# Differential attention: PE's shared-bank work placed between a slot's diagonal and its later scores

## The chip, the core and the metric

The kernel runs on one core of a Trainium2 chip. Its engines are PE (matmul), ACT (activation functions), DVE and POOL (elementwise work) and SP (which starts the DMAs); each takes its instructions in program order, and they wait for each other by semaphores. The metric is the device time of the whole kernel in microseconds, as a median of several runs; lower is better.

## What is computed

The reference is a stack of four layers over x of shape (16, 512, 128): differential attention, a grouped-query attention with a mixture of experts, eight blocks of linear attention, and a ternary feed-forward layer. Only the first is touched by the change:

```python
B, T, D = x.shape                      # 16, 512, 128; nh = 16, hd = 8
q = (x @ Wq.T).reshape(B, T, 2, nh // 2, hd)
k = (x @ Wk.T).reshape(B, T, 2, nh // 2, hd)
v = (x @ Wv.T).reshape(B, T, nh // 2, 2 * hd)
q, k = (_rms_norm(q), _rms_norm(k))
q, k = (_apply_rotary(q, cos, sin), _apply_rotary(k, cos, sin))
y1 = _causal_attn(q[:, :, 0], k[:, :, 0], v, scale)
y2 = _causal_attn(q[:, :, 1], k[:, :, 1], v, scale)
y = (y1 - lambda_full * y2).reshape(B, T, D)
return y @ Wproj.T
```

with x layer-normalised before and the result added to it. `_causal_attn` is softmax attention with a causal mask.

## The kernel before

`diff_attention` handles 16 batches of 512 tokens. The 16 heads of a batch are taken two at a time, so a batch has 8 slots, m = 0 to 7, and slot n = 8b + m + 1 of the whole stage is worked on in pass m of batch b. The scores of a slot are held transposed (keys on the partitions), in blocks of 128 by 128 at or above the causal diagonal:

- `score_diagonal(n)` (L1402, L1404) makes the eight diagonal blocks into two PSUM banks, SX. It waits until ACT has taken SX's last contents (`probs_x`).
- `score_later(n)` (L1416 to L1427) makes the remaining blocks, six matmuls, into three banks, SY. It waits for `probs_y`, that is for ACT's exponentials of the slot before.
- ACT: `exp_diagonal(n)` (L1566) and `exp_later(n)` (L1571) write exp of SX and of SY into a ring of six slots, PT. POOL masks the diagonal blocks (L1649).
- `weigh` (L1439) multiplies PT with V into the bank O, for a group of two slots: the blocks off the diagonal at even m, the diagonal ones at odd m. DVE copies O out (`copy_o`, L1822).

All else that needs PSUM goes through the two banks of M, the shared banks. A slot has one or two such uses on PE. Batch b's attention runs beside the projections of batches b + 1 and b + 2 (c and c2 in the code) and the output of batch b - 1 (p):

| m | PE's uses of M |
|---|---|
| 0 | `project_ks(c)` L1261, `turn_o2(p)` L1298 |
| 1 | `sum_q(c)` L1273, L1274 |
| 2 | `sum_k(c)` L1283, L1284, `turn_o3(p)` L1298 |
| 3 | `project_v(c)` L1291 |
| 4 | `turn_y(p)` L1341, `turn_o0(b)` L1298 |
| 5 | `project_out(p)` L1349, `turn_x(c2)` L1232 |
| 6 | `project_q(c2)` L1239, `turn_o1(b)` L1298 |
| 7 | `project_k(c2)` L1246, `project_qs(c2)` L1254 |

ACT empties some of these uses in an order of its own, written out by hand: `square` (L1526) in m = 6 and 7 and `rms` (L1532, L1535, Ln and Exp) in m = 1 and 2 stand between `exp_diagonal` and `exp_later`; `copy_v` (L1542, m = 3), `copy_yT` (L1548, m = 4) and `copy_xT` (L1520, m = 5) stand behind `exp_later`. The uses wait for their banks: `turn_y` for `copy_v`, `project_out` for `copy_yT`, `project_q` for `copy_xT`, `turn_x` for the combine of the group 0 on DVE (L1830), `turn_o2` for the sines on DVE (L1747). DVE's order is fixed as well: sines, combine(p,2), measure, `copy_o(p,3)`, splitting of q (L1754 to L1765), combine(p,3), splitting of k, `copy_o(b,0)`, centre (L1731), combine(b,0), `add_out`, and so on.

Of the kernel before, what the change touches and what calls it, by code (L numbers as in the profile page):

```python
# [1086 lines left out]
def diff_attention(nc, C, XT, G, NB):  # L1087
# [13 lines left out]
    with ExitStack() as ctx:  # L1101
# [119 lines left out]
        def pe_program(pe):  # L1221
# [35 lines left out]
            def project_ks(c):  # L1257
                if c:
                    pe.wait_ge(cos_done[K], c + 1)
                    pe.wait_ge(sq_ready[K], c + 1)  # L1260
                pe.matmul(lead(c, 1), w[:, 3, :], xnT[:, :], start=True, stop=True  # L1261
                          ).then_inc(turned_filled[K], 1)

            def sum_q(c):
                if c:
                    pe.wait_ge(sin_done[Q], c + 1)
                else:
                    pe.wait_ge(heads_ready, 1)
                    pe.wait_ge(sq_ready[Q], 1)
                if c >= 2:  # L1270
                    pe.wait_ge(o_used, 4 * (c - 2) + 3)
                pe.wait_ge(sq_split[Q], c + 1)
                pe.matmul(lead(c, 2), heads[:, :], sqs[:, 0, Q, :], start=True, stop=False)  # L1273
                pe.matmul(lead(c, 2), heads[:, :], sqs[:, 1, Q, :], start=False, stop=True  # L1274
                          ).then_inc(ss_filled[Q], 1)

            def sum_k(c):
                if c:
                    pe.wait_ge(ss_taken[Q], c + 1)
                else:  # L1280
                    pe.wait_ge(sq_ready[K], 1)
                pe.wait_ge(sq_split[K], c + 1)
                pe.matmul(lead(c, 3), heads[:, :], sqs[:, 0, K, :], start=True, stop=False)  # L1283
                pe.matmul(lead(c, 3), heads[:, :], sqs[:, 1, K, :], start=False, stop=True  # L1284
                          ).then_inc(ss_filled[K], 1)
# [25 lines left out]
            def turn_o1(b):  # L1311
                if b:
                    pe.wait_ge(out_done, b)
                else:
                    pe.wait_ge(v_taken, 2)
                turn_o(b, 1)

            def turn_o2(p):
                if p + 2 <= NB:
                    pe.wait_ge(sin_done[Q], p + 3)  # L1320
                else:
                    pe.wait_ge(o_used, 4 * p + 2)
                turn_o(p, 2)
# [40 lines left out]
            def g_project_qs():  # L1364
                pe.wait_ge(o_used, 4 * (NB - 2) + 2)
                pe.matmul(M[:, 1, :], G["wq"][:, 1, :], xnT[:, :], start=True, stop=True
                          ).then_inc(turned_filled[Q], 1)

            def g_sum_k():
                pe.wait_ge(sin_done[Q], NB + 1)  # L1370
                pe.wait_ge(o_used, 4 * (NB - 2) + 3)
                pe.wait_ge(g_kk_done, 1)
                pe.matmul(M[0:32, 1, :], G["pair_sum"][:, :], rotK, start=True, stop=True
                          ).then_inc(g_k_summed, 1)
# [9 lines left out]
            def operands(n, i):  # L1384
                pair, par = n % 8, (n // 8) % 2
                return (qT[64 * i:64 * i + KR, par, pair, :], kT[64 * i:64 * i + KR, par, pair, :])

            def score_diagonal(n):

                if n % 4 == 0:  # L1390
                    pe.wait_ge(loaded[Q][n // 4 % 2], 32 * (n // 8 + 1))
                    pe.wait_ge(loaded[K][n // 4 % 2], 32 * (n // 8 + 1))
                if n:
                    pe.wait_ge(probs_x, n)
                else:
                    pe.wait_ge(cos_done[K], 1)
                    pe.wait_ge(sq_ready[K], 1)
                    pe.wait_ge(sin_done[K], 1)
                (qa, ka), (qb, kb) = operands(n, 0), operands(n, 1)
                for j in range(NT):  # L1400
                    t = slice(j * P, (j + 1) * P)
                    pe.matmul(SX[:, 0, t], ka[:, t], qa[:, t], start=True, stop=True,  # L1402
                              skip_group_check=True)
                    last = pe.matmul(SX[:, 1, t], kb[:, t], qb[:, t], start=True, stop=True,  # L1404
                                     skip_group_check=True)
                last.then_inc(x_ready, 1)

            def score_later(n):

                if n:  # L1410
                    pe.wait_ge(probs_y, n)
                else:
                    pe.wait_ge(ss_taken[K], 1)
                    pe.wait_ge(v_taken, 1)
                (qa, ka), (qb, kb) = operands(n, 0), operands(n, 1)
                pe.matmul(SY[:, 1, 0:256], ka[:, P:2 * P], qa[:, 2 * P:SEQ], start=True, stop=True,  # L1416
                          skip_group_check=True).then_inc(shared_half, 1)
                pe.matmul(SY[:, 2, 0:384], kb[:, 0:P], qb[:, P:SEQ], start=True, stop=True,
                          skip_group_check=True)
                pe.matmul(SY[:, 0, 0:384], ka[:, 0:P], qa[:, P:SEQ], start=True, stop=True,  # L1420
                          skip_group_check=True)
                pe.matmul(SY[:, 2, 384:512], kb[:, 2 * P:3 * P], qb[:, 3 * P:SEQ], start=True,
                          stop=True, skip_group_check=True)
                pe.matmul(SY[:, 0, 384:512], ka[:, 2 * P:3 * P], qa[:, 3 * P:SEQ], start=True,
                          stop=True, skip_group_check=True)
                pe.wait_ge(shared_half, n + 1)
                pe.matmul(SY[:, 1, 256:512], kb[:, P:2 * P], qb[:, 2 * P:SEQ], start=True, stop=True,  # L1427
                          skip_group_check=True).then_inc(y_scored, 1)
# [31 lines left out]
            for b in range(NB + 1):  # L1460
                p, c, c2 = b - 1, b + 1, b + 2
                tail, now, then, next_but_one = b >= 1, b < NB, c < NB, c2 < NB
                for m in range(8):
                    n = 8 * b + m + 1
                    group = 4 * b + m // 2 - 1
                    weighing = 0 <= group < 4 * NB
                    if n < 8 * NB:
                        score_diagonal(n)
                        score_later(n)
                    if m == 0 and then:  # L1470
                        project_ks(c)
                    if m == 0 and tail:
                        turn_o2(p)
                    if m == 1 and then:
                        sum_q(c)
                    if m == 2 and then:
                        sum_k(c)
                    if m == 2 and c == NB:
                        g_sum_k()
                    if m == 2 and tail:  # L1480
                        turn_o3(p)
                    if m == 3 and then:
                        project_v(c)
                    if m == 3 and c == NB:
                        g_project_v()
                    if m == 4 and tail:
                        turn_y(p)
                    if m == 4 and now:
                        turn_o0(b)
                    if m == 5 and tail:  # L1490
                        project_out(p)
                    if m == 5 and c2 <= NB:
                        turn_x(c2)
                    if m == 6 and next_but_one:
                        project_q(c2)
                    if m == 6 and c2 == NB:
                        g_project_q()
                    if m == 6 and now:
                        turn_o1(b)
                    if m == 7 and next_but_one:  # L1500
                        project_k(c2)
                        project_qs(c2)
                    if m == 7 and c2 == NB:
                        g_project_kk()
                        g_project_qs()
                    if weighing and m % 2 == 0:
                        pe.wait_ge(probs_y, 2 * group + 2)
                        if group:
                            pe.wait_ge(o_copied, group)
                        weigh(group, EARLY[0] + EARLY[1])  # L1510
                    if weighing and m % 2 == 1:
                        pe.wait_ge(masked, 2 * group + 2)
                        weigh(group, DIAG[0] + DIAG[1]).then_inc(av_ready, 1)
# [2355 lines left out]
```

## Time and profile before

| | us |
|---|---|
| median of 3 runs | 3155.96 (3155.24 to 3159.12) |
| profiled execution | 3165.76 |
| its span, first to last instruction | 3164.0 |
| PE busy | 2882.8 (91% of the span) |
| DVE busy | 2482.6 (78%) |
| ACT busy | 2326.2 (74%) |
| POOL busy | 2104.2 (67%) |
| mean granted clock of PE | 0.954 |

The stage of the change is the first one; its last addition to x ends at 523.48 us. The other stages are the same code in both kernels. A timeline row gives the start, the length, the engine and line, and in brackets the time for which the engine did nothing before the instruction, with the instruction that ended the wait.

### The profile page before, as it was taken

Reading aid. Unit: us, or ns where it says so; the run is one execution under the profiler, and the core shown is the slowest. Engines: PE = TensorE matmul, PEld = TensorE weight load, DVE = VectorE, ACT = ScalarE, POOL = GpSimd, SP = SyncE. Lnnn points to the kernel's source line nnn. Section 1 sums busy time; section 2 is a strip of 40 time slices with the busy share of each in tenths; the row PEclk is TensorE's granted clock in tenths of the full one; section 3 lists DMA queues with packets and bytes.
Section 4 is the critical chain, followed back from the end, with each engine's and each line's share of the span. In section 5 each row is a group of like instructions: output and inputs, shape, how many; then the busy total and the mean of one; then the engine's idle time right before and its main releaser. Section 6 shows DMA issues by size and latency. Waiting matters only on the chain. (4 is left out here: it accounts for less than half of the span.)

```text
span 3164.0 us, 66212 instructions
## 1 busy us (share of the span) xinstructions
PE 2882.8 (91%) x22258; PEld 1871.3 (59%) x22258; DVE 2482.6 (78%) x6944; ACT 2326.2 (74%) x3601; POOL 2104.2 (67%) x2402
## 2 busy tenths in 40 slices
PE   6999997788998888789579999999999999999979
PEld 3555554344444444678246666666666666666668
DVE  5777776788888875567468888888888888888867
ACT  5888883466666667444289999999999999999833
POOL 5666673346555543577657888788877888788745
PEclk8999997799999999899789999999999999999989
DMA  4544534223322330685400000000000000000001
GB/s 121 131 108 112 129 92 91 59 62 69 69 57 60 72 70 19 191 271 158 128 1 1 17 1 17 1 7 11 6 12 1 17 1 17 1 17 1 1 14 41
DMA packets 151509, 178.31 MB, mean 56 GB/s; under 512 B 18619, under 2 KB 122784, under 8 KB 151076
## 3 DMA queue, kind: packets, MB, share of 16 engines
q1 hardware_dynamic: 142084, 157.14, 19.2%
q0 software_dynamic: 9088, 16.94, 1.6%
q8 instruction: 179, 2.93, 0.4%
q14 instruction: 158, 1.29, 0.1%
HBM read 99.82 MB, written 75.95 MB: 56 GB/s over the span
## 5 line engine op out<-in xcount | busy, mean ns | idle before, releaser
L3380 PE MATMUL lb_FF<-lb_h,lb_w 128*128 128x512 f32 x1024 | 502.0, 592 | 0.0
L3609 DVE TENSOR_SCALAR lb_z<-lb_M,lb_mv,lb_rstd 128x128 f32<-128x128 f32 x1024 | 344.9, 398 | 3.3 <-POOL lb_rstd L3534 3.0
L3497 ACT ACTIVATE lb_h<-lb_H,lb_prm 128x512 f32<-128x512 f32 x512 | 327.5, 699 | 2.6 <-PE lb_H L3371 2.6
L3534 POOL TENSOR_TENSOR lb_rstd<-lb_rstd,half 128x4 f32<-128x4 f32 x256 | 260.8, 1019 | 37.2 <-issue 1.3
L3365 PE MATMUL lb_H<-lb_x1s,lb_w 128*128 128x512 f32 x512 | 273.0, 533 | 0.0
L3380 PEld LDWEIGHTS lb_FF<-lb_h,lb_w 128*128 128x128 f32 x1024 | 193.5, 189 | 89.9 <-issue 61.1
L3601 DVE BATCH_NORM_STATS2 lb_stats<-lb_M 128x6 f32<-128x128 f32 x1024 | 226.9, 284 | 15.5 <-PE lb_M L3324 9.0
L1649 POOL TENSOR_SCALAR_AFFINE_SELECT da_PT<-da_PT 128x1024 f32<-128x1024 f32 x128 | 149.1, 1165 | 133.4 <-ACT da_PT L1566 133.3
L3366 PE MATMUL lb_H<-lb_x1s,lb_w 128*128 128x512 f32 x512 | 203.3, 397 | 0.0
L3371 PE MATMUL lb_H<-lb_x1s,lb_w 128*128 128x512 f32 x512 | 202.7, 397 | 0.1
L3552 POOL CAST lb_x1s<-lb_x 128x512 fp32r<-128x512 f32 x128 | 78.3, 611 | 173.7 <-DVE lb_x L3634 173.7
L2631 POOL DMA_INDIRECT moe_ys<-moe_y,moe_dest x156 | 159.0, 1019 | 50.5 <-issue 44.9
L794 DVE TENSOR_REDUCE ga_bm<-ga_S 128x8 f32<-128x1024 f32 x128 | 156.5, 1222 | 42.5 <-PE ga_S L379 41.4
L791 DVE TENSOR_REDUCE ga_bm<-ga_S 128x8 f32<-128x1024 f32 x128 | 156.0, 1219 | 42.4 <-PE ga_S L379 41.8
L1571 ACT ACTIVATE da_PT<-da_SY 128x1536 f32<-128x1536 f32 x128 | 184.8, 1443 | 0.0
L1566 ACT ACTIVATE da_PT<-da_SX 128x1024 f32<-128x1024 f32 x128 | 131.0, 1023 | 67.4 <-PE da_SX L1404 67.1
L3545 POOL TENSOR_TENSOR lb_xs<-H,lb_xs 128x512 fp32r<-128x512 f32 x126 | 167.8, 1332 | 18.1
L3555 POOL TENSOR_TENSOR lb_x1s<-lb_x,lb_x1s 128x512 fp32r<-128x512 f32 x128 | 163.5, 1277 | 20.8 <-issue 20.8
L3566 POOL TENSOR_TENSOR lb_y<-lb_ao,H 128x512 f32<-128x512 f32 x128 | 165.4, 1292 | 16.0 <-ACT lb_ao L3484 14.0
L1439 PE MATMUL da_O<-da_PT,da_V 128*32 128x128 f32 (+2 forms) x3584 | 174.6, 335 | 0.0
L3578 POOL TENSOR_TENSOR lb_y<-lb_ff,lb_x 128x512 f32<-128x512 f32 x128 | 165.1, 1290 | 8.5 <-PE lb_M L3324 5.3
L3478 ACT ACT_TABLE_LOAD x131 | 168.1, 1283 | 2.3
(514 smaller groups left out, 8860.8 us busy)
## 6 DMA issues: line engine op xcount, KB each, us to landing
moe_w<-experts_dram SPq DMA_DIRECT2D x39, 384.0 KB, 3.2
da_qT<-da_stq SPq DMA_DIRECT2D x64, 192.0 KB, 4.1
da_kT<-da_stk SPq DMA_DIRECT2D x64, 192.0 KB, 3.8
moe_x<-moe_xs SPq DMA_DIRECT2D x39, 260.0 KB, 3.6
tc_g<-moe_ys SPq DMA_DIRECT2D x32, 256.0 KB, 3.5
ga_q<-ga_stq SPq DMA_DIRECT2D x20, 384.0 KB, 5.8
lb_split<-moe_parts SPq DMA_DIRECT2D x8, 896.0 KB, 6.4
da_stq<-da_parts SPq DMA_DIRECT2D x16, 384.0 KB, 2.4
```

Source lines behind the costliest of these rows:

```text
L1439: last = pe.matmul(O[32 * c:32 * c + 32, q0:q0 + cols], V[:, (n // 4) % 2, j, 2 * (n % 4) + c % 2, :], PT[:, (2 * n + c // 2) % RING, c % ...
L1571: act.activation(PT[:, n % RING, :, 512:HEAD_COLS], SY[:, :, :].rearrange("p a n -> p (a n)").rearrange("p (i n) -> p i n", i=2), ACT.Exp, ...
L3365: pe.matmul(H[:, k % 2, :], w1[:, 0, k, :], x1s[:, 0, :], start=True, stop=False)
L3366: pe.matmul(H[:, k % 2, :], w1[:, 1, k, :], x1s[:, 0, :], start=False, stop=False)
L3371: pe.matmul(H[:, k % 2, :], w1[:, 0, k, :], x1s[:, 1, :], start=False, stop=True).then_inc(h_filled, 1)
L3380: pe.matmul(FF[:, :], w2[:, k, :], h[:, k, :], start=(k == 0), stop=(k == KC - 1)).then_inc(ff_filled, 1)
L3478: act.preload_act_table_set("gelu_apprx_tanh_and_others")
L3497: act.activation(h[:, k, :], H[:, k % 2, :], ACT.Gelu_apprx_tanh, bias=col(FB1 + k, i)).then_inc(h_ready, 1)
L3534: pool.tensor_tensor(out[:, :], out[:, :], C["half"][:, 0:NT], ALU.pow).then_inc(done, 1)
L3545: pool.tensor_tensor(part_of_x(i, 1), state(i), part_of_x(i, 0).bitcast(F32), ALU.subtract).then_inc(xs_ready, 1)
L3601: v.bn_stats(stats[:, t, :], M[:, t * P:(t + 1) * P])
L3609: last = v.tensor_scalar(z[:, t, :], M[:, t * P:(t + 1) * P], mv[:, t, 0:1], rstd[:, t:t + 1], ALU.subtract, ALU.mult)
```

## The change

In each slot `score_later(n)` moves from directly behind `score_diagonal(n)` to behind the slot's uses of M; `weigh` stays last. ACT, DVE, POOL and SP keep their orders.

```diff
--- before.py
+++ after.py
@@ -1466,7 +1466,6 @@
                     weighing = 0 <= group < 4 * NB
                     if n < 8 * NB:
                         score_diagonal(n)
-                        score_later(n)
                     if m == 0 and then:
                         project_ks(c)
                     if m == 0 and tail:
@@ -1503,6 +1502,8 @@
                     if m == 7 and c2 == NB:
                         g_project_kk()
                         g_project_qs()
+                    if n < 8 * NB:
+                        score_later(n)
                     if weighing and m % 2 == 0:
                         pe.wait_ge(probs_y, 2 * group + 2)
                         if group:
```

In m = 5 of a batch, PE's rows were (L1404 ends the diagonal scores, L1349 is `project_out`, L1232 is `turn_x`, L1439 is `weigh`):

```order
L1404 MATMUL da_SX<-da_qT,da_kT 128x128
L1416 MATMUL da_SY<-da_qT,da_kT 128x256
L1418 MATMUL da_SY<-da_qT,da_kT 128x384
L1420 MATMUL da_SY<-da_qT,da_kT 128x384
L1422 MATMUL da_SY<-da_qT,da_kT 128x128
L1424 MATMUL da_SY<-da_qT,da_kT 128x128
L1427 MATMUL da_SY<-da_qT,da_kT 128x256
L1349 MATMUL da_M<-da_wout,da_yT 128x128 x4
L1232 MATMUL da_M<-ident,da_xn 128x128 x4
L1439 MATMUL da_O<-da_PT,da_V 32x128 x16
```

and are now:

```order
L1404 MATMUL da_SX<-da_qT,da_kT 128x128
L1349 MATMUL da_M<-da_wout,da_yT 128x128 x4
L1232 MATMUL da_M<-ident,da_xn 128x128 x4
L1416 MATMUL da_SY<-da_qT,da_kT 128x256
L1418 MATMUL da_SY<-da_qT,da_kT 128x384
L1420 MATMUL da_SY<-da_qT,da_kT 128x384
L1422 MATMUL da_SY<-da_qT,da_kT 128x128
L1424 MATMUL da_SY<-da_qT,da_kT 128x128
L1427 MATMUL da_SY<-da_qT,da_kT 128x256
L1439 MATMUL da_O<-da_PT,da_V 32x128 x16
```

The six later scores moved behind `project_out` and `turn_x`.

In m = 2, from the last of the later scores to the first of `weigh` (`sum_k`, L1283 and L1284, and `turn_o3`, L1298):

```order
L1427 MATMUL da_SY<-da_qT,da_kT 128x256
L1283 MATMUL da_M<-da_sqs,da_heads 128x512
L1284 MATMUL da_M<-da_sqs,da_heads 128x512
L1298 MATMUL da_M<-ident,da_oT 128x128 x4
L1439 MATMUL da_O<-da_PT,da_V 32x384 x4
```

and now, from the last of the diagonal scores to the first of the later ones:

```order
L1404 MATMUL da_SX<-da_qT,da_kT 128x128
L1283 MATMUL da_M<-da_sqs,da_heads 128x512
L1284 MATMUL da_M<-da_sqs,da_heads 128x512
L1298 MATMUL da_M<-ident,da_oT 128x128 x4
L1416 MATMUL da_SY<-da_qT,da_kT 128x256
```

`sum_k` and `turn_o3` now stand ahead of the wait that the first later score (L1416) has.

ACT from the norm of m = 2 to the copy of m = 5, the same in both kernels (L1532 and L1535 are the Ln and Exp of the norm, L1542, L1548 and L1520 the three copies):

```order
L1532 ACTIVATE da_rs<-da_M,rms_eps 128x512
L1535 ACTIVATE da_rs<-da_rs 128x512
L1571 ACTIVATE da_PT<-da_SY 128x2x768
L1566 ACTIVATE da_PT<-da_SX 128x2x512
L1571 ACTIVATE da_PT<-da_SY 128x2x768
L1542 ACTIVATE da_V<-da_M 128x32x16
L1566 ACTIVATE da_PT<-da_SX 128x2x512
L1571 ACTIVATE da_PT<-da_SY 128x2x768
L1548 ACTIVATE da_yT<-da_M 128x512
L1566 ACTIVATE da_PT<-da_SX 128x2x512
L1571 ACTIVATE da_PT<-da_SY 128x2x768
L1520 ACTIVATE da_xnT<-da_M 128x512
```

Nothing moved here: each copy stands behind the later exponentials (L1571) of its slot.

## Rows read from the trace of the kernel before

**Rows 1.** Busy times: two neighbouring batches, then thirteen. Columns: stretch, length; PE, PEld, DVE, ACT, POOL busy; clock; DMA.
```profile
270.65:300.02 29.37, 26.82 (x389) 16.73 (x388) 22.20 (x42) 24.11 (x26) 19.57 (x18) 1.00 0.44 117
240.51:270.65 30.14, 28.23 (x389) 17.25 (x388) 21.50 (x42) 24.23 (x26) 19.46 (x18) 0.94 0.46 117
62.79:449.86 387.07, 357.21 (x5045) 220.99 (x5044) 283.79 (x533) 314.20 (x326) 253.84 (x234) 0.97 0.45 115
```
**Rows 2.** Waits on PE, 60 to 450 us: in total, times, longest (us).
```profile
PE da_SY L1416 <- ACT da_PT L1571: 23.8, 20, 1.5
```
**Rows 3.** Timeline of PE: start us, length us, instruction [idle before it].
```profile
268.31 0.63 PE L1232 MATMUL da_M<-ident,da_xn 128*128 128x128 f32 x4 [0.42 <-DVE da_u L1830]
...
270.65 1.12 PE L1239 MATMUL da_M<-da_xnT,da_w 128*128 128x512 f32 x2
...
279.03 0.60 PE L1298 MATMUL da_M<-ident,da_oT 128*128 128x128 f32 x4
...
282.43 1.08 PE L1439 MATMUL da_O<-da_PT,da_V 128*32 128x128 f32 x32
...
285.33 0.28 PE L1416 MATMUL da_SY<-da_qT,da_kT 48*128 48x256 bf16 x1 [1.49 <-ACT da_PT L1571]
...
289.44 0.28 PE L1416 MATMUL da_SY<-da_qT,da_kT 48*128 48x256 bf16 x1 [0.63 <-ACT da_PT L1571]
...
289.99 1.16 PE L1291 MATMUL da_M<-da_w,da_xnT 128*128 128x128 f32 x8
...
292.87 0.66 PE L1341 MATMUL da_M<-ident,da_y 128*128 128x128 f32 x4
...
293.89 1.50 PE L1439 MATMUL da_O<-da_PT,da_V 128*32 128x384 f32 x24
...
297.68 0.63 PE L1232 MATMUL da_M<-ident,da_xn 128*128 128x128 f32 x4 [0.42 <-DVE da_u L1830]
...
298.24 1.08 PE L1439 MATMUL da_O<-da_PT,da_V 128*32 128x128 f32 x32
```
**Rows 4.** Timeline of ACT in the same batch.
```profile
281.43 1.03 ACT L1566 ACTIVATE da_PT<-da_SX 128x1024 f32<-128x1024 f32 x1 [1.34 <-PE da_SX L1404]
...
282.54 0.69 ACT L1532 ACTIVATE da_rs<-da_M,rms_eps 128x512 f32<-128x512 f32 x1
...
283.84 1.43 ACT L1571 ACTIVATE da_PT<-da_SY 128x1536 f32<-128x1536 f32 x1
...
289.28 1.02 ACT L1566 ACTIVATE da_PT<-da_SX 128x1024 f32<-128x1024 f32 x1
...
290.19 1.45 ACT L1571 ACTIVATE da_PT<-da_SY 128x1536 f32<-128x1536 f32 x1
...
291.52 0.61 ACT L1542 ACTIVATE da_V<-da_M 128x512 f32<-128x512 f32 x1
...
298.35 0.60 ACT L1520 ACTIVATE da_xnT<-da_M 128x512 f32<-128x512 f32 x1 [0.21 <-PE da_M L1232]
```
**Rows 5.** Timeline of DVE in this batch and the one before.
```profile
253.44 0.69 DVE L1822 COPY da_oT<-da_O 128x512 f32<-128x512 f32 x1
...
262.86 0.69 DVE L1822 COPY da_oT<-da_O 128x512 f32<-128x512 f32 x1 [1.83 <-PE da_O L1439]
...
277.42 0.69 DVE L1822 COPY da_oT<-da_O 128x512 f32<-128x512 f32 x1 [0.51 <-PE da_O L1439]
...
278.03 0.68 DVE L1747 TENSOR_TENSOR da_rotB<-da_M,da_rope 128x512 f32<-128x512 f32 x1
...
283.58 0.69 DVE L1822 COPY da_oT<-da_O 128x512 f32<-128x512 f32 x1
...
284.19 0.78 DVE L1754 TENSOR_TENSOR da_rotA<-da_rotA,da_rs 128x512 f32<-128x512 f32 x1
...
289.00 1.64 DVE L1754 TENSOR_TENSOR da_rotA<-da_rotA,da_rs 128x512 f32<-128x512 f32 x1
...
292.23 0.69 DVE L1822 COPY da_oT<-da_O 128x512 f32<-128x512 f32 x1 [0.36 <-PE da_O L1439]
```

## The prediction

> **What bounds the kernel now.** I first read which part of the span the change can touch: only the first stage, differential attention, to about 524 us of the 3164.0 us span. There I took the busy times of single batches [rows 1]. In a batch without any half-clock stretch PE is busy 26.82 of 29.37 us, ACT 24.11, DVE 22.20, POOL 19.57. No engine is full, so order and waits set the length. Then I read who waits for whom on PE [rows 2]: one wait is large, the later scores of a slot (L1416) for the exponentials of the slot before (L1571), 23.8 us in 20 places, the longest 1.5 us. The timelines of one clean batch on PE, ACT and DVE [rows 3 to 5] show where it is. I number the slots of a batch m = 0 to 7; a batch of shared-bank work is followed from m = 6 (project_q, L1239) to the next m = 6. The wait falls in m = 2 (285.33, idle 1.49) and m = 3 (289.44, idle 0.63), and one smaller wait, of 0.42 us, in m = 5, where turn_x (L1232) waits for DVE (297.68). Everywhere else PE runs without a pause.
>
> Why just m = 2: in m = 1 and 2 ACT has the norm's Ln and Exp (1.30 us from 282.54 to 283.84) in front of L1571, so the exponentials run late, and PE stands with its shared-bank uses of m = 2 still to do. The change puts those uses into that wait. So far it looks like a gain; what has to be counted is what the same order does in the other six slots, where PE didn't wait.
>
> **The change, step by step.** No instruction is added or removed. In every slot the later scores (0.55 us of PE, from 289.44 to 289.99) go behind the slot's shared-bank uses. The other pieces of a slot are the weighting matmuls (1.01 or, on even m, 1.43: 1.08 of row 298.24 and 1.50 of row 293.89, less the 0.07 by which the last one runs on) and the diagonal scores (0.22, what is left of the 2.34 between 268.31 and 270.65 after 0.56, 1.01 and 0.55), so a slot starts 0.77 before its first shared-bank use in the old order. I carry the clean batch through the new order, starting at the turn_x of 268.31, which stays where it is, and keep "shift" for new time minus old time. A result of PE or ACT reaches a waiting engine 0.05 us after its end (the 0.63 us turn of 297.68 ends at 298.31, the copy starts at 298.35).
>
> m = 5 to 6. Old: ACT does L1571 of m = 5 while PE waits for turn_x, so copy_xT follows the turn at once, and project_q starts 2.34 us after turn_x (268.31 to 270.65). New: the later scores stand behind turn_x, ACT's L1571 behind them, and copy_xT behind L1571, as ACT's order is unchanged. That is 0.56 (297.68 to 298.24) + 0.63 until the scores are out (their 0.55 and a run-on of 0.08) + 0.05 + 1.33 (290.19 to 291.52) + 0.60 + 0.05 = 3.22 us. Shift of project_q: +0.88, and PE idles in m = 6, where it did not.
>
> m = 7 only carries this: uses +0.88, weighting matmuls and next slot +1.43, since the scores now lie behind the uses. The DVE copies of O therefore come 1.43 late.
>
> m = 0. turn_o2 (old 279.03) needs sines(Q), which DVE does behind copy_o: copy at 277.42 + 1.43, sines 0.61 later and 0.69 long, so 280.20, against 279.91 by PE alone. Shift +1.17. The slot after it starts +1.72.
>
> m = 1. The first exponentials start at 281.43 + 1.72 = 283.15; 0.91 later (289.28 to 290.19) Ln and Exp, whose sums are there by then, 1.30, so L1571 at 285.36 (old 283.84, +1.52), its end (1.43 long) visible at 286.84. PE's weighting matmuls start at 282.43 + 1.17 + 0.55 = 284.15 and end so that m = 2 starts at 285.16; copy_o(p,3), old 283.58, also shifts by 1.72 and starts at 285.30.
>
> m = 2. Here the gain is. sum_k and turn_o3 run inside the wait; the later scores start at 286.84, then directly the weighting matmuls: 286.84 + 0.55 + 1.43 = 288.82 for m = 3. The old start of m = 3 is 289.99 - 0.55 - 0.63 (the idle time) - 0.4 (diagonal scores to their last end) = 288.41. The shift has gone from +1.72 to +0.41: 1.31 us back. On ACT the diagonal exponentials of m = 2 follow L1571 at 286.69, and L1571 of m = 2 comes 0.91 + 1.30 later, at 288.90; its 1.44 end, visible, at 290.39.
>
> m = 3. project_v lies inside the wait, the later scores start at 290.39 (old 289.44), and with 0.55 and 1.01 m = 4 starts at 291.95, old 292.10: 0.56 more back. PE is level with the old order here.
>
> m = 4. turn_y must wait for copy_v, since it writes the bank of M that copy_v reads. ACT's copy_v stands behind L1571 of m = 3, which starts 0.91 after the one of m = 2 has let ACT go (288.90 + 1.33): 291.14; copy_v at 292.47, 0.61 long, visible 293.13; PE is ready at 292.17. In the old order copy_v ended at 292.13 and turn_y was at 292.87, with the later scores ahead of it. Cost 0.96. With 1.02 for both turns (292.87 to 293.89), 0.55 and 1.43, m = 5 starts at 296.13.
>
> m = 5. The same on ACT: copy_yT stands behind L1571 of m = 4, whose scores now come behind turn_y and turn_o0 (294.15), so 0.68 later L1571, 294.83 + 1.33 + 0.60 + 0.05 = 296.81 for project_out, PE ready at 296.35: 0.46 idle. project_out takes 1.09, like project_v (289.99, 1.16 with the run-on). It ends at 297.90: by PE and ACT alone turn_x is at +0.22.
>
> DVE decides last. turn_x needs the combine behind centre, and DVE's work from copy_o(p,3) on has no pause that it must have. Its length without its own idle time is 14.10 - 0.36 = 13.74 us in the clean batch (283.58 to 297.68), and 14.87 - 1.83 = 13.04 in the one before (253.44 to 268.31) [rows 3, 5]. From 285.30 this gives 298.34 to 299.04, so +0.66 to +1.36 per batch. The spread comes from DVE instructions that run beside POOL: L1754 took 0.78 us at 284.19 and 1.64 us at 289.00. I take +0.9, nearer to the shorter chain, since the shorter chain was measured where POOL's mask of m = 3 came at another moment than in the clean batch, as it will in the new order too.
>
> The number of batches is 14 (turn_x for 2 to 15): 14 x 0.9 = +12.6; ends 14 x 0.66 = +9.2 and 14 x 1.36 = +19.0. The transfers between batches are no term: their stores hang on DVE's splits, shifted by the same 1 to 2 us, and the loads are used two slots or more later.
>
> The clock. From the first of 13 whole batches to the last (62.79 to 449.86) 387.07 us passed; 13 x 29.37 would be 381.8. The 5.3 us more are in batches like the second of [rows 1], 30.14 us at a mean clock of 0.94 (2.4 GHz with a stretch at 1.2). The half-clock stretch comes right behind the 1.5 us wait of m = 2. The new order breaks that wait up: the largest left is 0.95. I credit two thirds of the 5.3, -3.5; bounds 0 and -5.3 (PE stands 3.2 us per batch in the new order by the steps above, against 2.5 in the old, which argues against the whole).
>
> Sum: +12.6 - 3.5 = **+9.1 us**. The profiled execution of before took 3165.76 us (span 3164.0 and 1.8 around it), so its like would take 3174.9. That execution is 0.3% above the median of the timed ones, 3155.96; on the median I predict **3165 us**.
>
> The Trainium skill ("SBUF — State Buffer", section "SBUF: two separate sides") says that DVE and POOL share one port pair under an exclusive lock, and the later one blocks fully. The 1.64 against the 0.78 us of the L1754 at 284.19 agrees. By this rule the chain could also lose its blocked pieces in the new phase; then DVE would be out of the way, which is the second rival.
>
> The same skill ("TensorE: Matmul & The Clock Gate", section "What's actually happening") says that the slow clock is the default and activity releases it. By that rule a fuller m = 2 keeps the clock and a broken-up batch may lose it elsewhere; the traces here show only the first half.
>
> **Rivals.**
> 1. Faster. The 1.31 + 0.56 us regained in m = 2 and 3 stay, because the waits of m = 4 and 6 for ACT's copies don't bind: 14 x 1.87 = -26, with the clock about -30: 3126 us; half of it would be 3141. For it: this is PE's one large wait [rows 2]. Against: three copies on ACT (copy_v, copy_yT, copy_xT) stand behind L1571 in the same program order. Chance 0.07.
> 2. No difference. DVE's chain falls below the PE and ACT path (+0.22) or the clock gives all 5.3 us back: 14 x 0.22 - 5.3 = -2.2, 14 x 0.66 - 5.3 = +3.9: 3154 to 3160. For it: 0.86 us of the clean chain is the one long L1754 (1.64 against 0.78). Chance 0.27.
> 3. Forecast, +5 to +16: 3161 to 3172. Chance 0.53.
> 4. Much slower. A DVE instruction more is caught beside POOL (another 0.86, as 1.64 against 0.78): +1.36 + 0.86 = +2.2 per batch, 14 x 2.2 - 3.5 = +27: 3183. It decides as soon as the chain is longer than 13.74. Chance 0.13.
>
> What this kernel's timing can tell from no change is about 0.2%, 6.3 us. Rivals 2 and the low end of 3 lie within it: faster 0.07, same 0.30, slower 0.63. Range 3153 to 3179: it leaves out rival 1 and the far part of rival 4.
>
> **What would show it.** Right: PE's wait at L1416 shrinks to some 0.3 us in m = 2 and 3; new waits at turn_y (L1341) for ACT L1542 of 0.9 us and at project_q (L1239) for ACT L1520 of 0.9 us, 14 or so each; turn_x still waits for DVE; ACT now waits before L1571 for L1427, which it hardly did; batches of 30.0 to 30.8 us. Wrong: no wait at L1239, batches under 29.4, or half-clock stretches as frequent as before with batches at 30.3 (then only the clock term fails). If POOL's or DVE's mean durations change by more than 0.1 us each, the DVE term is the one that was mis-sized.

## The result: slower by 0.45%, and the profile after

| | before | changed |
|---|---|---|
| median of 5 runs each, us | 3156.47 | 3170.68 |
| lowest to highest | 3155.24 to 3161.16 | 3170.28 to 3179.54 |
| ratio | | 1.0045 (95%: 1.0029 to 1.006) |
| profiled execution, span | 3164.0 | 3177.8 |
| batch without half-clock stretch | 29.37 | 30.69 |
| thirteen batches | 387.07 | 399.95 |
| last addition of the stage starts | 522.8 | 535.4 |

The change costs 14.2 us; 3165 was predicted, with 3153 to 3179 as the range. The interval of the ratio means 9 to 19 us, so the forecast of +9.1 lies at its low end. Of the 13.8 us by which the spans differ, 12.6 lie in the first stage.

A clean batch and the thirteen whole batches of the changed kernel, to be laid beside [rows 1] (stretch, length; PE, PEld, DVE, ACT, POOL busy; clock; DMA):

```profile
307.02:337.71 30.69, 28.14 (x389) 16.56 (x389) 21.34 (x41) 23.89 (x26) 18.95 (x18) 1.00 0.46 114
60.51:460.46 399.95, 366.58 (x5045) 215.53 (x5045) 277.17 (x534) 310.66 (x326) 246.58 (x234) 1.00 0.44 112
```

PE executes the same instructions as in 26.82 busy us before, and the profile counts as much idle time in both batches (29.37 - 26.82 = 2.55 and 30.69 - 28.14 = 2.55). So the whole 1.32 us of the longer batch stand as busy. I read them as waits all the same: a row's length runs on past the moment at which the next instruction could have started, and where PE has to wait, that run-on hides a part of it. The turn_y of 298.19 below is followed 1.01 us later by turn_o0, of which the profile calls 0.38 idle. In the old order the distance was 0.49 us (292.87 to 293.36):

```profile
293.36 0.60 PE L1298 MATMUL da_M<-ident,da_oT 128*128 128x128 f32 x4
```

The clock over thirteen batches is 1.00 where it was 0.97. No half-clock stretch starts in them any more; only the end of one reaches into the first (60.51, mean clock 0.97, 31.57 us long). The stage is longer all the same.

Who waits for whom on PE, 62 to 462 us (us in all, times, longest), against [rows 2]. From 1506 on, lines are one higher than before, so L1572 is the L1571 of before, L1543 the L1542, L1521 the L1520:

```profile
PE da_M L1341 <- ACT da_V L1543: 11.3, 13, 0.9
PE da_M L1239 <- ACT da_xnT L1521: 8.9, 13, 0.7
PE da_M L1298 <- DVE da_oT L1823: 5.0, 12, 0.7
PE da_M L1349 <- ACT da_yT L1549: 3.5, 13, 0.3
PE da_M L1232 <- DVE da_u L1831: 3.2, 13, 0.3
PE da_SY L1416 <- ACT da_PT L1572: 0.3, 1, 0.3
```

The one large wait is gone (0.3 us instead of 23.8), and there are five others, one of each in nearly every batch, which before were not there or were one of 0.42 us. They add up to 31.9 us. Before, all that the profile lists added up to 29.6 (23.8, 5.5 at turn_x and 0.3), so the sum alone would not show the loss: the hidden parts of the waits are missing in it. On ACT the wait has changed sides:

```profile
ACT da_PT L1572 <- PE da_SY L1427: 73.7, 65, 1.8
ACT da_PT L1567 <- PE da_SX L1404: 8.2, 26, 0.3
```

Before, ACT waited 51.5 us for the diagonal scores and not at all for the later ones. Now it waits 73.7 us for the later scores.

PE's timeline of one clean batch, first the turn_x that starts it, then the later scores and uses of M from m = 2 on, to be laid beside [rows 3]:

```profile
273.13 0.63 PE L1232 MATMUL da_M<-ident,da_xn 128*128 128x128 f32 x4 [0.25 <-DVE da_u L1831]
...
291.82 0.28 PE L1416 MATMUL da_SY<-da_qT,da_kT 48*128 48x256 bf16 x1
...
295.36 0.28 PE L1416 MATMUL da_SY<-da_qT,da_kT 48*128 48x256 bf16 x1
...
298.19 0.63 PE L1341 MATMUL da_M<-ident,da_y 128*128 128x128 f32 x4 [0.87 <-ACT da_V L1543]
299.20 0.63 PE L1298 MATMUL da_M<-ident,da_oT 128*128 128x128 f32 x4 [0.38 <-DVE da_oT L1823]
...
302.40 1.16 PE L1349 MATMUL da_M<-da_wout,da_yT 128*128 128x128 f32 x8 [0.27 <-ACT da_yT L1549]
303.81 0.63 PE L1232 MATMUL da_M<-ident,da_xn 128*128 128x128 f32 x4 [0.25 <-DVE da_u L1831]
304.37 0.28 PE L1416 MATMUL da_SY<-da_qT,da_kT 48*128 48x256 bf16 x1
...
307.02 1.13 PE L1239 MATMUL da_M<-da_xnT,da_w 128*128 128x512 f32 x2 [0.69 <-ACT da_xnT L1521]
```

In m = 2 and 3 the later scores start without a stop of PE that the profile shows. Each use of M from turn_y in m = 4 to project_q in m = 6 has a wait. The length of each slot, from its first diagonal score to that of the next slot, shows where the batch wins and loses:

| us | m = 6 | 7 | 0 | 1 | 2 | 3 | 4 | 5 | batch |
|---|---|---|---|---|---|---|---|---|---|
| before, from 269.88 | 3.70 | 3.71 | 3.71 | 2.44 | 4.97 | 3.68 | 3.23 | 3.93 | 29.37 |
| changed, from 305.93 | 4.57 | 3.80 | 4.06 | 2.55 | 3.58 | 3.12 | 4.83 | 4.18 | 30.69 |

m = 2 and 3 give 1.95 us back, m = 4 loses 1.60, m = 6 0.87, and the other four 0.80 together. On ACT, the same batch as the timeline above:

```profile
296.10 1.45 ACT L1572 ACTIVATE da_PT<-da_SY 128x1536 f32<-128x1536 f32 x1
297.43 0.61 ACT L1543 ACTIVATE da_V<-da_M 128x512 f32<-128x512 f32 x1
...
300.41 1.45 ACT L1572 ACTIVATE da_PT<-da_SY 128x1536 f32<-128x1536 f32 x1 [1.46 <-PE da_SY L1427]
301.76 0.59 ACT L1549 ACTIVATE da_yT<-da_M 128x512 f32<-128x512 f32 x1
...
305.03 1.45 ACT L1572 ACTIVATE da_PT<-da_SY 128x1536 f32<-128x1536 f32 x1 [1.76 <-PE da_SY L1427]
306.37 0.59 ACT L1521 ACTIVATE da_xnT<-da_M 128x512 f32<-128x512 f32 x1
```

Each copy (297.43, 301.76, 306.37) stands directly behind the later exponentials of its slot, and these had to wait 1.46 and 1.76 us for scores that PE makes last. And on DVE, from copy_o(p,3) to combine, beside [rows 5]:

```profile
290.36 0.69 DVE L1823 COPY da_oT<-da_O 128x512 f32<-128x512 f32 x1 [1.97 <-PE da_O L1439]
290.97 1.33 DVE L1755 TENSOR_TENSOR da_rotA<-da_rotA,da_rs 128x512 f32<-128x512 f32 x1
...
293.68 1.37 DVE L1766 CAST da_parts<-da_rotB 128x512 bf16<-128x512 f32 x1
...
296.36 1.57 DVE L1755 TENSOR_TENSOR da_rotA<-da_rotA,da_rs 128x512 f32<-128x512 f32 x1
...
298.37 0.68 DVE L1823 COPY da_oT<-da_O 128x512 f32<-128x512 f32 x1
...
300.25 2.75 DVE L1732 TENSOR_SCALAR da_xn<-XT,da_mv,da_rstd 128x128 f32<-128x128 f32 x4
```

DVE has no idle time here between 290.36 and turn_x at 303.81: 13.45 us, between the 13.04 and 13.74 of before.

### The profile page after: what moved, and what is told of

It reads as the page before. It is cut to its first block and busy times, and to the rows that moved or that the text cites. A ratio compares the mean times of both kernels' runs of the same rounds, so it can differ in the third digit from the quotient of the medians.

```text
span 3177.8 us, 66212 instructions
## 1 busy us (share of the span) xinstructions
PE 2891.9 (91%) x22258; PEld 1864.3 (59%) x22258; DVE 2473.5 (78%) x6944; ACT 2322.1 (73%) x3601; POOL 2094.2 (66%) x2402
## 5 line engine op out<-in xcount | busy, mean ns | idle before, releaser
L1572 ACT ACTIVATE da_PT<-da_SY 128x1536 f32<-128x1536 f32 x128 | 185.2, 1447 | 92.2 <-PE da_SY L1427 92.1
L1650 POOL TENSOR_SCALAR_AFFINE_SELECT da_PT<-da_PT 128x1024 f32<-128x1024 f32 x128 | 141.8, 1108 | 144.5 <-ACT da_PT L1567 144.5
L3567 POOL TENSOR_TENSOR lb_y<-lb_ao,H 128x512 f32<-128x512 f32 x128 | 165.1, 1290 | 16.3 <-ACT lb_ao L3485 14.2
L1439 PE MATMUL da_O<-da_PT,da_V 128*32 128x128 f32 (+2 forms) x3584 | 167.4, 325 | 0.0
```

The source lines that it names most:

```text
L1439: last = pe.matmul(O[32 * c:32 * c + 32, q0:q0 + cols], V[:, (n // 4) % 2, j, 2 * (n % 4) + c % 2, :], PT[:, (2 * n + c // 2) % RING, c % ...
L1572: act.activation(PT[:, n % RING, :, 512:HEAD_COLS], SY[:, :, :].rearrange("p a n -> p (a n)").rearrange("p (i n) -> p i n", i=2), ACT.Exp, ...
```

## The experiments

The time of the kernel before varied between 3153 and 3171 us over the chips on which these ran, so each run is read by its ratio to the runs of before on its own chip, and by its batch: the distance between two project_q starts without a half-clock stretch. It is 29.37 us before and 30.69 with the change. In most runs it repeats within 0.03 us. In f1, f2 and f3 it does not, because there PE also waits up to 1.4 us at the diagonal scores of m = 7: the 28.75 and 28.76 of f1 and f3 are the three batches of thirteen without that wait and without a half-clock stretch, and for f2 the middle one is given. So the thirteen whole batches of each profiled execution stand beside it, with the number of them that have a half-clock stretch of their own.

| run | batch, us | thirteen, us | with half clock | ratio to before (95%) |
|---|---|---|---|---|
| before | 29.37 | 387.07 | 6 | 1 |
| the change | 30.69 | 399.95 | 0 | 1.0045 (1.0029 to 1.0060) |
| e1, moved in m = 2, 3 | 29.83 | 392.27 | 3 | 1.0008 (0.9993 to 1.0023) |
| e2, moved in m = 5 | 30.29 | 398.09 | 5 | 1.0047 (1.0031 to 1.0062) |
| e3, moved in all but m = 5 | 29.38 | 383.45 | 1 | 0.9995 (0.9979 to 1.0011) |
| e4, change, copy_xT ahead | 29.92 | 389.91 | 1 | 1.0021 (1.0005 to 1.0037) |
| e8, moved in m = 7, 0 | 29.82 | 396.34 | 10 | 1.0027 (1.0017 to 1.0036) |
| f4, moved in m = 4 | 29.37 | 388.34 | 7 | 0.9992 (0.9980 to 1.0004) |
| f1, before, short mask | 28.75 | 384.79 | 7 | 0.9953 (0.9934 to 0.9971) |
| e6, change, short mask | 29.68 | 386.09 | 0 | 0.9975 (0.9962 to 0.9987) |
| e5, m = 2, 3, short mask | 27.57 | 359.54 | 0 | 0.9882 (0.9864 to 0.9901) |
| e7, m = 2, 3, third later | 29.83 | 392.58 | 3 | 1.0010 (0.9999 to 1.0022) |
| f3, before, centre early | 28.76 | 381.93 | 5 | 0.9994 (0.9980 to 1.0008) |
| f2, m = 2, 3, centre early | 28.43 | 371.45 | 0 | 0.9951 (0.9938 to 0.9964) |

### Which slots gain and which lose

Theory: the gain is in m = 2 and 3, the loss where ACT's copies follow the later exponentials. The five runs below differ from before only in the slots in which the scores are moved:

```diff
                     if n < 8 * NB:
                         score_diagonal(n)
-                        score_later(n)
+                        if not (m in (2, 3)):
+                            score_later(n)
...
+                    if n < 8 * NB and (m in (2, 3)):
+                        score_later(n)
                     if weighing and m % 2 == 0:
```

with `m == 5` in e2, `m != 5` in e3, `m in (7, 0)` in e8 and `m == 4` in f4.

**e1, m = 2 and 3 alone.**

> The later scores are moved only in m = 2 and 3, where PE waited. Theory (the gain and the loss sit in different slots): m = 2 and 3 give back 1.3 + 0.5 us, of which the waits of DVE and of ACT's copies behind them take about half, since turn_x hangs on DVE's chain; a batch takes 28.5 us (29.37 before), 14 x 0.9 = 12.6 us, and the half-clock stretches of the stage go as well, 5 us: 3139 us, between 3134 and 3146. Rival (any use of M ahead of the scores makes the exponentials late, or the chain on DVE sets the batch whatever PE does): no batch shorter than 29.3 us, 3151 us or more.

A batch of 29.83 us, longer than before and far from 28.5; the time itself does not differ clear of noise (1.0008). The rival was right in its second half, that DVE's chain sets the batch. PE's largest wait in this run:

```profile
PE da_M L1232 <- DVE da_u L1833: 20.6, 13, 1.6
```

1.6 us in each of 13 batches at turn_x. DVE and POOL in one batch show why (lines are two or three higher than before: L1757 is L1754, L1762 L1759, L1734 L1731, L1645 L1642, L1652 L1649). DVE:

```profile
252.71 0.69 DVE L1825 COPY da_oT<-da_O 128x512 f32<-128x512 f32 x1
...
258.14 1.64 DVE L1757 TENSOR_TENSOR da_rotA<-da_rotA,da_rs 128x512 f32<-128x512 f32 x1
259.88 1.14 DVE L1762 CAST da_parts<-da_rotA 128x512 bf16<-128x512 f32 x1
...
262.82 3.64 DVE L1734 TENSOR_SCALAR da_xn<-XT,da_mv,da_rstd 128x128 f32<-128x128 f32 x4
```

POOL at the same time:

```profile
258.05 1.19 POOL L1645 TENSOR_TENSOR da_parts<-da_rotB,da_parts 128x512 bf16<-128x512 f32 x1
259.21 1.52 POOL L1652 TENSOR_SCALAR_AFFINE_SELECT da_PT<-da_PT 128x1024 f32<-128x1024 f32 x1
262.99 1.19 POOL L1645 TENSOR_TENSOR da_parts<-da_rotB,da_parts 128x512 bf16<-128x512 f32 x1 [2.25 <-DVE da_parts L1768]
264.13 2.25 POOL L1652 TENSOR_SCALAR_AFFINE_SELECT da_PT<-da_PT 128x1024 f32<-128x1024 f32 x2
```

The cast of 259.88 took 1.14 us beside a mask (0.43 when alone), the product of 258.14 took 1.64 beside `third` (0.80 in the other place of the same batch), and the four instructions of centre took 3.64 beside `third` and two masks, where they took 2.75 before. The chain from copy_o(p,3) (252.71) to turn_x (267.27) is 14.56 us long without a pause. By gaining on PE and ACT in m = 2 and 3 the kernel moved a second mask onto centre. The gain could not come through in any case but by a shorter chain: from turn_x (237.44) to copy_o(p,3) it is 15.27 us, as before, for m = 2 and 3 do not lie in this part, and 15.27 + 14.56 = 29.83.

**e2, m = 5 alone.**

> Moved only in m = 5, behind turn_x. Theory: project_q waits for copy_xT, which stands behind the later exponentials (L1571), whose scores now stand behind turn_x: +0.88 us per batch, batch 30.2 to 30.4 us, half-clock stretches as before, 14 x 0.9 = +12.6: 3169 us. Rival (no single slot costs; the loss is the sum of small delays on DVE beside POOL): under +0.3 per batch, 3156 to 3160.

30.29 us, as the theory had it: +0.92 per batch. The wait at turn_x is 0.87 in place of 0.42, and that of m = 2 is as large as before:

```profile
PE da_M L1232 <- DVE da_u L1833: 11.3, 13, 0.9
...
PE da_SY L1416 <- ACT da_PT L1574: 27.0, 34, 1.5
```

**e3, all slots but m = 5.**

> The change in every slot but m = 5. Theory: the wait of project_q goes (0.7 to 0.9 us), turn_x still comes late by DVE's chain: batch 29.4 to 29.8 us against 30.69, with the half-clock stretches gone 3151 to 3158 us. Rival (DVE's chain alone sets the batch of the change): the batch stays near 30.7 and the time near 3170.

29.38 us, at the edge of what was expected: 1.31 less than the change. Without the move in m = 5 the clean batch is as long as before, and the time is too (0.9995): the 1.95 us that m = 2 and 3 give back are lost in the other slots, most of them (1.60) in m = 4. The profile shows no wait at turn_x, but DVE still releases it: turn_x follows the end of the combine by 0.15 us as in the change, and 15.92 (264.67 to 280.59) + 13.45 (280.59 to 294.04) = 29.37.

**e8, m = 7 and 0 alone.**

> Moved only in m = 7 and 0. Theory: turn_o2 waits for the sines behind the late copy_o, and every slot whose diagonal scores are followed by a use of M takes 0.08 us longer on PE: +0.35 us per batch, 29.7 us, ratio 1.001 to 1.002 with the half-clock stretches as before. Rival (nothing is lost outside m = 4 to 6): batch 29.4, ratio 1.000.

A clean batch is 29.82 us, a little over the expected 29.7. But the time rose by more than that, 1.0027 where at most 1.002 was expected. The granted clock over the stage:

```profile
62.00:462.00 400.00, 372.14 (x5097) 224.25 (x5092) 267.21 (x536) 318.37 (x329) 247.22 (x235) 0.96 0.45 114
```

The half-clock stretch that follows the wait of m = 2 came in 10 of the 13 batches instead of 6, and such batches are 30.6 us long. That part was not expected.

**f4, m = 4 alone.**

> Moved only in m = 4. In the whole change PE waits 0.87 us at turn_y for copy_v. Theory: that wait exists only because PE comes early out of m = 2 and 3; alone, copy_v has ended when PE comes, so batch 29.3 to 29.5 us and ratio 0.999 to 1.001. Rival (the slot costs by itself, as m = 5 does): batch 30 or more.

29.37 us: no loss, and at turn_y only four waits of at most 0.2 us. The wait of 0.87 us at turn_y exists only where PE comes out of m = 2 and 3 early.

### The copy on ACT

**e4, the whole change with copy_xT ahead.**

```diff
+                    if m == 5 and c2 <= NB:
+                        copy_xT(c2)
                     if n < 8 * NB:
                         exp_later(n)
...
-                    if m == 5 and c2 <= NB:
-                        copy_xT(c2)
```

> The whole change, with ACT's copy_xT of m = 5 ahead of that slot's later exponentials. Theory: the copy follows the turn at once, project_q starts 0.7 us earlier than in the change, batch 29.9 to 30.0 us (30.69), 3158 to 3161 us. Rival (what costs is that the scores themselves stand behind turn_x, whatever the copy does): batch 30.5 or more, 3168 or more.

29.92 us: 0.77 of the 1.32 us is the one copy that stands behind exp_later. The rival is out. The ratio, 1.0021, has a wide interval (1.0005 to 1.0037).

### How much is DVE beside POOL

The mask of a slot was cut to one block of four in three kernels (three of four diagonal blocks stay unmasked):

```diff
                 d = PT[:, n % RING, :, 0:512].rearrange("p i (j q) -> p i j q", j=NT)
-                pool.affine_select(d, d, [[0, 2], [0, NT], [1, P]], ALU.is_ge, 0.0, base=0,
+                d = d[:, :, 0, :]
+                pool.affine_select(d, d, [[0, 2], [1, P]], ALU.is_ge, 0.0, base=0,
```

**e5, m = 2 and 3 alone.**

> Moved only in m = 2 and 3, and POOL masks one of the four diagonal blocks of a slot (the other three stay unmasked: part of the computation is left out). Theory: in m = 2 and 3 alone, the batch of 29.83 us is DVE's chain from copy_o(p,3) to turn_x, 14.57 us long, in which centre takes 3.64 us beside two masks of POOL and the split of k 1.64 + 1.14 beside other POOL work. With short masks the chain is 12.5 to 13.5 us, turn_x hardly waits, batch 28.3 to 28.9 us; ratio to before 0.992 to 0.996. Rival (something else than DVE beside POOL holds turn_x back): batch 29.5 or more, ratio 0.999 or more.

27.57 us and 0.9882, below the expected 28.3 and 0.992. The split of k runs at 0.68 and 0.43 us and centre at 2.06. This is the largest effect of the study: 2.26 us per batch against e1.

**e6, the whole change.**

> The whole change with the same short mask (three of four diagonal blocks unmasked). Theory: DVE's waits at turn_o0 (0.38) and turn_x (0.25) go, the waits for ACT's copies (copy_v, copy_yT, copy_xT) stay: batch 30.0 to 30.3 us against 30.69, ratio to before 1.001 to 1.003. If the whole loss were DVE beside POOL, the batch would fall under 29.4 and the ratio below 1.0.

29.68 us, 0.3 below what was expected, so the collisions weigh more than I thought. The ratio missed too: 0.9975, under 1, where 1.001 to 1.003 was expected; what that means can only be said with the control, f1. The slot m = 4 falls from 4.83 to 4.25 us, as turn_o0 no longer waits for DVE. But the waits for ACT's copies are all still there, unchanged in size:

```profile
PE da_M L1341 <- ACT da_V L1543: 11.3, 13, 0.9
PE da_M L1239 <- ACT da_xnT L1521: 8.9, 13, 0.7
PE da_M L1349 <- ACT da_yT L1549: 3.5, 13, 0.3
```

**f1, the kernel before.**

> The kernel before with the short mask (one of four diagonal blocks masked), the control for the two runs with it, whose batches are 29.68 us (the whole change) and 27.57 us (m = 2 and 3 alone). Theory: before, DVE was hardly in the way (0.42 us at turn_x), and the half-clock stretches stay: batch 28.8 to 29.1 us. Then the order of the whole change costs 0.6 to 0.9 us per batch with DVE out of the way, and the order in m = 2 and 3 gives 1.2 to 1.5 us. Rival (without the collisions on DVE the whole change is no loss): batch 29.6 or more.

28.75 us in a clean batch. So with the collisions reduced the whole change still costs 29.68 - 28.75 = 0.93 us of its 1.32 in clean batches, and the move in m = 2 and 3 alone gains 28.75 - 27.57 = 1.18.

For the time this is weaker. Only three of the thirteen batches of f1 are clean: seven have a half-clock stretch, and in seven PE waits up to 1.3 us at the diagonal scores; e6 has neither. All thirteen take 384.79 us in f1 and 386.09 in e6, 1.3 us apart, where with whole masks they are 12.9 apart. The intervals of the two ratios, 0.9953 (to 0.9971) and 0.9975 (from 0.9962), overlap. That the order alone makes the kernel slower with short masks is therefore shown for the clean batch and not for the time.

**e7, another place for `third`.** As e1, and POOL's third(c, K) is put behind the mask of m = 4 (`if m == 3 and c < NB` becomes `m == 4`).

> Moved only in m = 2 and 3, and POOL's third(c, K) comes behind the mask of m = 4 instead of the mask of m = 3. POOL waited 2.25 us for the split of k with that mask's data ready; now it masks in that time. Theory: centre meets one POOL instruction less, 2.75 us instead of 3.64, batch 28.9 to 29.0 us, ratio 0.996 to 0.998. Rival: the batch stays at 29.8, or the later third makes the transfers of k late (a wait of PE for them in m = 7).

29.83 us, as in e1. The collision was not avoided but moved. DVE in this run:

```profile
293.33 1.61 DVE L1766 TENSOR_TENSOR da_rotB<-da_rotA,da_parts 128x512 f32<-128x512 f32 x1
...
295.36 2.73 DVE L1734 TENSOR_SCALAR da_xn<-XT,da_mv,da_rstd 128x128 f32<-128x128 f32 x4
```

Centre takes 2.73 us, as hoped, but now the subtraction in front of it (L1766) takes 1.61 instead of 0.69, because it meets the mask that was brought forward.

### A version that beats both

In f2 and f3 DVE measures and centres x one batch earlier, in the idle time that it has around project_q and project_k, so that centre is no longer between copy_o(p,3) and turn_x.

```diff
                 if now:
                     copy_o(b, 1)
+                if b + 3 < NB:
+                    measure(b + 3)
                 if next_but_one:
                     cosines(c2, Q)
                 if now:
                     combine(b, 1)
+                if b + 3 < NB:
+                    centre(b + 3)
                 if next_but_one:
                     cosines(c2, K)
```

The old places keep only what runs beside batch 0; POOL's rsqrt_stats goes to m = 6, and the load of x behind store_q of the batch two earlier.

**f2, with the scores moved in m = 2 and 3.**

> Moved only in m = 2 and 3, and DVE measures and centres the x of a batch one batch earlier, in its idle time of m = 6 and 7 (with POOL's rsqrt behind the mask of m = 6 and the load of x earlier), so that centre is not between copy_o(p,3) and turn_x. Nothing is left out. Theory: that chain falls from 14.57 to about 11 us and turn_x waits no more; batch 27.9 to 28.4 us against 29.37 before; with 14 batches and 5 us of half clock 16 to 25 us saved, ratio 0.992 to 0.996. Rival: centre in m = 7 holds back cosines(c2, K), and with it project_ks and copy_o(b, 2), by as much: batch 29 or more.

**f3, with the scores not moved.**

> The same early centre in the kernel before, later scores not moved, the control for the run above. Theory: only the 0.42 us at turn_x can go, the waits of m = 2 and 3 stay: batch 29.0 to 29.3 us, ratio 0.998 to 1.000. Then most of the gain of the run above is the move of the scores.

f2 is the fastest kernel of the study that computes everything: 0.9951 of before, 0.994 to 0.996, and the only one of those whose interval lies clear of 1 on this side. f3 has three clean batches of 28.76 us, better than the 29.0 expected, but its time is at 0.9994: the wait of m = 2 is still there, five batches have a half-clock stretch, and eight have a wait of up to 1.0 us at the diagonal scores. Over thirteen batches f3 takes 381.93 us and f2 371.45, so 29.38 and 28.57 per batch: with centre out of the way the move in m = 2 and 3 gives 0.81 us per batch. How much of it is clock and how much waiting can't be told from the clean batches, since f2 has only one without the wait at the diagonal scores (27.80 us; the others run from 28.04 to 29.24). In f2 centre's four instructions take 1.12 us in all but one of the thirteen, where DVE meets no POOL instruction:

```profile
292.08 1.12 DVE L1736 TENSOR_SCALAR da_xn<-XT,da_mv,da_rstd 128x128 f32<-128x128 f32 x4
```

What PE waits for in f2:

```profile
PE da_SX L1402 <- issue: 9.8, 13, 1.4
PE da_SY L1416 <- ACT da_PT L1574: 8.6, 29, 0.3
PE da_M L1232 <- DVE da_u L1835: 2.8, 1, 2.8
```

turn_x waits once only, and behind the thirteen batches (2.8 us). What remains is up to 1.4 us at the diagonal scores in twelve of the thirteen, without a releaser in the profile. The loads of q and k are one candidate: a load of k was issued at 286.44 and such loads take 4.1 us to land, against diagonal scores at 292.67. This was not tested, and the cause stays open.

## Why the prediction was right

Direction, range and mechanism held; the size was 14 us where 9 were forecast. Step by step:

- **m = 5 to 6, copy_xT.** 3.22 us from turn_x to project_q were worked out; 303.81 to 307.02 is 3.21. e2 (+0.92) and e4 (-0.77) show it alone, e3 (-1.31) what the move in m = 5 costs in the whole change.
- **m = 2 and 3.** PE's wait for L1571 is gone as said. The steps put 1.31 + 0.56 us into the two slots; they are 1.39 + 0.56 shorter. e1 shows that the batch keeps nothing of it while DVE's chain is in the way. With short masks it keeps 1.18 (e5 against f1, clean batches).
- **m = 4.** turn_y's wait: 0.96 forecast, 0.87 measured. But the slot lost 1.60 us, not 0.96: the steps had no wait at turn_o0, which starts 1.01 us behind turn_y instead of 0.49, as it waits for DVE's copy_o(b,0). In e6, where DVE comes in time, the slot loses 1.02. project_out's wait, 0.46 forecast, is 0.27, as PE comes to it later. f4 confirms that turn_y's wait needs the early PE.
- **DVE decides last.** True, and here is the term that was mis-sized. PE and ACT alone were put at +0.22; e6, whose turn_x waits no more for DVE, is at 29.68 - 29.37 = +0.31. The chain was right: 13.45 us, inside the 13.04 to 13.74, though 0.17 longer than the 13.28 that +0.9 stands for. Its start was not: copy_o(p,3) follows turn_x by 290.36 - 273.13 = 17.23 us, 1.96 more than before (283.58 - 268.31 = 15.27), where 1.72 was worked out. Each slot in which a use of M follows the diagonal scores takes about 0.08 us more on PE (the first use stands 0.3 us behind the first diagonal score, where the later scores stood 0.23 behind it), three times between turn_x and copy_o. So 1.96 - 0.65 (14.10 - 13.45) = +1.31 per batch and not +0.9. The upper end, +1.36, held.
- **The clock.** -3.5 was credited, with -5.3 as the bound. In the thirteen batches no half-clock stretch starts any more, so the whole 5.3 came back and not two thirds: 1.8 us more than credited, which hid a part of the mis-sized term. Their sum: 13 x 1.32 - 5.3 = 11.9, measured 12.9. The last 1.0 is in two batches: 0.88 in the first (31.57 us), into which the end of a half-clock stretch reaches and whose project_q takes 2.01 us instead of 1.13, and 0.35 in one (31.04 us) whose turn_o0 waits 0.74 us for DVE instead of 0.38; one batch is 0.19 shorter.
- **DVE beside POOL.** The long DVE instructions (0.68 to 1.64, 0.43 to 1.14, 0.69 to 1.61 us) stand beside POOL's in every trace, and they shrink when POOL's masks do. The rule of the Trainium skill ("SBUF — State Buffer", section "SBUF: two separate sides") that the later one is blocked agrees with this. The instructions' mean durations hardly moved (DVE 0.53 to 0.52 us, POOL 1.08 to 1.05), so the sign that was named for a mis-sized DVE term, 0.1 us, did not show, though the term was mis-sized: its error was in the start of the chain. The second rival did not come: DVE lost pieces (the cast of k, 0.43) and got others (the cast of 293.68, 1.37).

Of the rivals, the first (the gain of m = 2 and 3 stays) is refuted by the waits at L1341 and L1239 and by e1. The fourth, a longer chain that locks in, did not come in the change but is just what e1 shows: 14.56 us.

## What to carry to other kernels

Moving a wait's cover into it helps the slot that waits; before it is done in all slots, ask in each who consumes the work that is put last, and what stands behind that consumer in its own queue: here a 0.6 us copy behind a 1.4 us exponential cost 0.8 us of every batch. Where two engines slow each other, as DVE and POOL do here, an engine that starts earlier also collides elsewhere, so a gain on the critical engine must be laid against the other timelines. And two obstacles to one gain have to be taken away together: the move in m = 2 and 3 alone (e1, 1.0008) and the early centre alone (f3, 0.9994) changed the time by nothing clear of noise, both together (f2) by -0.49%.

## What the runs showed of the hardware that was not expected

- DVE's four centring instructions take 1.12 us with POOL quiet, 2.06 beside `third` and a short mask, 2.75 beside `third` and a whole one, and 3.64 beside `third` and two. Cutting three quarters of each of POOL's masks took 0.47% off the kernel before (f1).
- The clock: stretches at 1.2 GHz came in 6 of 13 batches before and in 10 of 13 in e8, both behind the 1.5 us wait in m = 2, and each lengthened its batch by about 0.8 us. In e1 they came in 3, with the 1.6 us wait at turn_x as the longest, and cost 1.5 us each. None began in the thirteen of the change and of e5, whose largest waits are 0.9 and 0.6 us; but e3 and e4 had one each with no wait over 0.9, and f2 none with waits of up to 1.4 us in twelve batches. So the length of the longest wait alone does not decide it, and what does was not found. e8 shows that the same wait can meet more stretches when another slot changes.
- A use of M that follows the diagonal scores starts 0.31 to 0.33 us after the first of them; the later scores started 0.23 after it.
